# A four-layer kernel's Mamba scan stage: order of dt's projection, D times u and the decays of paired states

## What is computed

```python
u, z = split(xn @ in_w.T)                # 256 channels each
u    = silu(causal_conv4(u) + conv_b)
dbc  = u @ xproj_w.T                     # 64 columns for dt, 16 for B, 16 for C
dt   = softplus(dbc[..., :64] @ dt_w.T + dt_b)
dA   = exp(dt[..., None] * A)            # A: 256 x 16
dBu  = (dt * u)[..., None] * B[:, :, None, :]
h    = dA * h + dBu                      # over time, for each of 16 states
y    = sum_n(h * C) + u * D
out  = (y * silu(z)) @ out_w.T
```

## Time and profile before

| | us |
|---|---|
| median of the runs | 1367.63 |
| the profiled execution, span | 1397.4 |
| scan stage in it, first times_c to the last instruction of GpSimd's part | 44.4 to 808.0 |
| PE, DVE, ACT, POOL busy, whole span | 1272.1, 1097.7, 947.2, 1013.4 |
| one full unit of the scan stage, from GpSimd's times_c(11) to the next | about 47.6 |
| 40.00 to 810.00: PE, DVE, ACT, POOL busy | 728.79, 726.25, 668.12, 742.17 |

### The profile page before, as it was taken

One profiled execution on the slowest core, in us unless ns is written; L12 is line 12 of the kernel. 1 busy time (PEld: TensorE's weight loads), 2 busy tenths in 40 slices (PEclk: granted clock), 3 DMA queues, 4 the chain that ended last, 5 costly groups with the idle time before them and its releaser, 6 DMA issues.

```text
span 1397.4 us, 27753 instructions
## 1 busy us (share of the span) xinstructions
PE 1272.1 (91%) x9894; PEld 962.1 (69%) x9894; DVE 1097.7 (79%) x1829; ACT 947.2 (68%) x1630; POOL 1013.4 (73%) x620
## 2 busy tenths in 40 slices
PE   6799999999999999999998779999989999986695
PEld 2567767676777676766766646689966666656693
DVE  5799999999999999999999953333357888874475
ACT  5888988898889888988988842245545555532243
POOL 2789999999999999999999916223334665664442
PEclk9999999999999999999999999999999999998798
DMA  5545434543444454444444351312152000021223
GB/s 187 145 131 161 138 139 118 161 149 129 139 139 165 133 150 139 164 132 152 139 146 111 114 216 47 90 44 86 56 157 86 2 1 1 13 64 34 79 72 100
DMA packets 153014, 154.73 MB, mean 111 GB/s; under 512 B 96624, under 2 KB 121712, under 8 KB 143168
## 3 DMA queue, kind: packets, MB, share of 16 engines
q1 hardware_dynamic: 148112, 143.16, 32.8%
q0 software_dynamic: 4768, 9.81, 2.2%
HBM read 138.66 MB, written 20.20 MB: 114 GB/s over the span
## 4 chain that ended last, share of the span: by engine, by line
PE 49%; ACT 21%; DVE 16%; issue 8%; another core or an unknown queue 2%; DMA 2%; POOL 1%; SPq 1%; DVEq 1%; POOLq 0%; ACTq 0%
DVE hh L887 7%; PE pq L410 6%; ACT da L720 6%; PE pa L506 4%; PE py L525 3%; ACT pa L725 3%; PE bank L1562 3%; PE bank L1558 2%; PE pr L2016 2%; PE bank L1572 2%; PE pr L2219 2%; PE pr L2030 2%; PE bank L1478 2%; DVE hh L897 2%
## 5 line engine op out<-in xcount | busy, mean ns | idle before, releaser
L1042 POOL TENSOR_TENSOR hc<-hh,cs 128x1024 f32<-128x1024 f32 x256 | 596.9, 2369 | 24.6 <-DVE hh L887 21.7
L887 DVE TENSOR_TENSOR_SCAN hh<-da,st,pa 128x512 f32<-128x512 f32 x240 | 292.7, 1261 | 14.1 <-PE pa L506 12.6
L525 PE MATMUL py<-ident,hc 128*128 128x128 f32 x2048 | 268.4, 277 | 7.4 <-ACT yt L738 5.8
L525 PEld LDWEIGHTS py<-ident,hc 128*128 128x128 f32 x2048 | 229.1, 141 | 54.4 <-issue 29.1
L506 PEld LDWEIGHTS pa<-dg,dtut 64*128 64x128 f32 x2560 | 160.9, 189 | 107.0 <-issue 103.2
L506 PE MATMUL pa<-dg,dtut 64*128 64x128 f32 x2560 | 189.8, 285 | 29.6 <-DVE hh L887 20.6
L720 ACT ACTIVATE da<-dt,w 128x512 f32<-128x512 f32 x320 | 209.7, 711 | 0.2
L897 DVE TENSOR_TENSOR_SCAN hh<-pa,st,hh 128x512 f32<-128x512 f32 x144 | 175.2, 1265 | 6.1 <-POOL hh L1032 3.7
L725 ACT ACTIVATE pa<-dt,w 128x512 f32<-128x512 f32 x192 | 124.5, 680 | 35.2 <-DVE hh L887 20.8
L410 PE MATMUL pq<-xn,w 128*128 128x512 f32 x248 | 124.6, 627 | 3.6 <-ACT xn L755 3.6
L1032 POOL TENSOR_TENSOR hh<-dtu,bs 128x1024 f32<-128x1024 f32 x48 | 112.8, 2365 | 3.1 <-issue 1.9
(11 more groups left out here) (341 smaller groups left out, 2643.8 us busy)
## 6 DMA issues: line engine op xcount, KB each, us to landing
cs<-bcrows SPq DMA_DIRECT2D x64, 1024.0 KB, 4.9
dg<-blocks SPq DMA_DIRECT2D x80, 256.0 KB, 5.0
bs<-bcrows SPq DMA_DIRECT2D x48, 256.0 KB, 3.7
blocks<-bcrows SPq DMA_DIRECT2D x320, 1.0 KB, 3.2
xsorted<-in_pads SPq DMA_DIRECT2D x13, 387.0 KB, 5.7
rot<-in_rot SPq DMA_DIRECT2D x4, 1024.0 KB, 4.9
wx<-in_l_w SPq DMA_DIRECT2D x4, 1024.0 KB, 10.0
ysort<-ytoken SPq DMA_DIRECT2D x14, 256.0 KB
```

The costliest lines, as they stand in the source:

```text
L525: i = pe.matmul(py[:, h * CH + kt * P:h * CH + (kt + 1) * P], hc[s % HCS][:, h, t], ident[:, :], is_transpose=True, start=n == 0 and kt == ...
L887: v.tensor_tensor_scan(hh[(NS * m + nj) % HHS][:, h, :], da[q % DAS][:, :], inflows, 0.0 if first else st[:, m % 2, nj, h:h + 1], ALU.mult ...
L1042: g.tensor_tensor(hc[s % HCS][:, :, :], hh[s % HHS][:, :, :], cs[j % 2][:, s % CG, :].unsqueeze(1).broadcast_to([P, HF, CH]), ALU.mult).th ...
```

## The change

D*u goes from step 13 of TensorE to step 7, and from step 12 of ScalarE to step 5. `dt_project` and `relu_abs` come one step earlier each. The decays of pairs count on a semaphore of their own (`s_da`, which later serves `pad_zeroed` too, with its counts raised by `zero0`), have eight tiles instead of four, and are written at places given by two tables: DECAYS_FIRST before prep, DECAYS_LATE behind it. ScalarE's order from step 4 on becomes: keep_sum; keep_rows; decays 5, 6; relu_abs first half; u_times_d; decays 7; relu_abs second half; decays 8, 9; sigmoid; square 1; decays 11; square 2; decays 10, 12; square 3; decays 14; relu_again; keep_pre; decays 13, 15.

```diff
+DECAYS_FIRST = {0: (1,), 1: (2, 3), 3: (4,), 6: (7,), 8: (11,), 9: (10,), 10: (12,), 11: (14,), 12: (13, 15), 15: (16,)}
+DECAYS_LATE = {4: (5, 6), 6: (8, 9)}
...
-SLOTS, DAS, BG = 4, 4, 2
+SLOTS, DAS, BG = 4, 8, 2
...
+        s_zero, zero0 = sem("pair_decayed_then_pad_zeroed"), UNITS * 4 * len(PAIRS)
...
+            s_da = s_zero
...
-                by_tensor = [item[0] == "y" for item in handed_items]
+                elsewhere = [item[0] in ("y", "flow") for item in handed_items]
...
-                DD_AT = 9
+                DD_AT = 3
...
(TensorE's prep)
-                            if n in (5, 6):
-                                dt_project(m, n - 5)
+                            if n in (4, 5):
+                                dt_project(m, n - 4)
...
(ScalarE's prep)
-                            if n in (6, 7):
-                                relu_abs(m, n - 6)
-                            if n == 7:
-                                sigmoid(m)
+                            if n in (5, 6):
+                                relu_abs(m, n - 5)
...
-                        if n == 12:
+                        if n == 5:
                             u_times_d(m - 1)
                         if m < UNITS:
-                            if n in (8, 9, 10):
-                                square(m, n - 8)
+                            if n in (7, 8, 10):
+                                square(m, (7, 8, 10).index(n))
...
-                                act.activation(da[q % DAS][:, :], dt[m % 2][:, h, :], ACT.Exp, scale=wd[m % 2][:, a:a + 1]).then_inc(s_slot, 1)
+                                act.activation(da[q % DAS][:, :], dt[m % 2][:, h, :], ACT.Exp, scale=wd[m % 2][:, a:a + 1]).then_inc(s_da, 1)
...
(ScalarE's loop over the steps)
-                        ahead = s + 1 < STEPS and by_pe(s + 1) and BY_P.index((s + 1) % NS) % 2 and (s + 1) % NS < 10
-                        if s + 1 < STEPS and not ahead:
-                            decays(s + 1)
+                        for n in DECAYS_FIRST.get(s % NS, ()):
+                            if s // NS * NS + n < STEPS:
+                                decays(s // NS * NS + n)
...
-                        if s % NS == PAIRS[0][0] - 1:
-                            decays(s + 2)
...
                         prep(s // NS + 1, s % NS)
+                        for n in DECAYS_LATE.get(s % NS, ()):
+                            decays(s // NS * NS + n)
+                        if s % NS == 6 and s // NS + 1 < UNITS:
+                            sigmoid(s // NS + 1)
...
-                        if s % NS in [own[0] - 1 for own in PAIRS[1:] if own[1] < 10]:
-                            decays(s + 2)
...
(VectorE's scan)
-                                v.wait_ge(s_slot, slot_count(i))
+                                v.wait_ge(s_da, q + 1)
```

More of the change, by code:

```diff
@@ L301, in layer0_mamba @@
                 turn = {item: i for i, item in enumerate(handed_items)}
-                by_tensor = [item[0] == "y" for item in handed_items]
+                elsewhere = [item[0] in ("y", "flow") for item in handed_items]
                 def slot_count(i):
-                    return i + 1 - sum(by_tensor[:i + 1])
+                    return i + 1 - sum(elsewhere[:i + 1])
                 def dt_count(m):
@@ L1202, in build @@
         s_ht, s_yo, s_ys = sem("hidden_made"), sem("y_made"), sem("y_kept")
-        s_zero = sem("pad_zeroed")
         routed = {"route": 0}
@@ L1623, in tiles_scalar @@
                     act.wait_ge(s_re, 32)
-                    act.wait_ge(s_zero, 1)
+                    act.wait_ge(s_zero, zero0 + 1)
                     kept_up(0)
@@ L1668, in tiles_vector @@
                     v.wait_ge(s_re, 32)
-                    v.wait_ge(s_zero, 1)
+                    v.wait_ge(s_zero, zero0 + 1)
                     kept_gate(0)
```

## The result

The kernel after takes 1388.16 us (median of 4 runs, 1383.78 to 1393.36), the kernel before 1366.33 (4 runs, 1364.85 to 1369.02): a ratio of 1.0154, 95% interval 1.0125 to 1.0184, or 21.8 us (17 to 25) slower. The forecast was 1381 with a range to 1387; the sign, the ring and its parts were right, the sum was 7 us short. The four runs of before in this batch are on the low side: 61 further runs of it have a median of 1368.7, and against that after is 19.5 us slower. The profiled execution of after took 1390.27 us, with a span of 1388.1 and a granted clock of 0.982.

The account below looks back on a forecast made before the run. The prediction took a GpSimd and VectorE ring of 47.6 us a unit as the bound, replaced after the change by ScalarE's at 48.55; 14 times +0.95, 13.3 us, on 1367.6 gave 1381 us, range 1371 to 1387.

Parts of the forecast that it names:

- the ring: Scan stage, ScalarE's decays of 1 to 10, VectorE's steps 10 and 11, then back: 48.55 us a unit against 47.6.
- the sum: Whole stage: 14 rings at +0.95 us each, 13.3 us, put on the median 1367.6, giving 1381.
- Three small terms ... They cancel: Stage total: +0.35 in unit 0, up to -0.7 for faster scans, up to +0.5 where those don't count; net nothing.
- term for unit 0: Unit 0 of the scan stage: +0.35 us, because the decays of 10 come late there too.
- term for the units with faster scans: Units where a sequence begins and scans carry no initial state: up to -0.7 us off the loss.
- T: Time from ScalarE's decays of step 1 to the end of the first relu_abs's abs: 15.84 us.
- the waits named for the changed profile: Expected: VectorE before step 10 (0.5 to 0.8 us) and step 6 (1.5), TensorE before second dt_project (0.7 to 1.0), GpSimd 2.
- ScalarE's ring ... 45.8, 1.8 us under the present unit: Kernel before: ScalarE's loop through the decays of 10 takes 45.8 us, leaving 1.8 us of slack under 47.6.
- All that ScalarE costs VectorE in it is ... 0.17: GpSimd and VectorE's loop, kernel before: VectorE waits 0.17 us for the decays of 9; gain at most 2.4 us.
- Rival D: TensorE idles in each unit and drops to its lower clock: another 1 us a unit, +28 us, 1395; chance 0.03.
- A's two prices: Bounds of the main forecast (chance 0.74): costlier draining before loads +0.2 us a unit; D*u freeing 1.04, better overlaps -0.3.
- E's further stall: Rival: one more stall of 0.3 to 0.5 us a unit in TensorE's steps 8 to 10, 1386; chance 0.06.

Follow-up runs that it names:

- after again: The changed kernel, unchanged, run and profiled a second time; 1387.77 us, one run.
- before again: The kernel before, unchanged, run and profiled a second time; 1363.96 us, one run.
- dt back: The changed kernel with dt_project, relu_abs, sigmoid and squares at their old steps; 1370.93 us, 1.0014 against the kernel before.
- the decays alone: The kernel before with only the pairs' own semaphore, eight tiles and new tables of decay steps; 1383.19 us, 1.0098 against the kernel before.
- the run with the decays of 10 first: The changed kernel with the decays of 10 written ahead of those of 11; 1387.08 us, one run.
- dt alone: The kernel before with only dt_project and relu_abs one step earlier; 1409.77 us, 1.0282 against the kernel before.
- before a third time: The kernel before, unchanged, run and profiled a third time; 1373.11 us, one run.

## Why the prediction was right and where it was wrong

The step that failed is the sum over the stage, "Three small terms ... They cancel", and not the ring. Its term for unit 0 was +0.35 and measured 2.0; its term for the units with faster scans was up to -0.7 and came out at +0.8; and a time that goes with a lower granted clock was no term of it at all.

- **The ring was right, by its mechanism.** 48.55 forecast, 48.62 to 48.65 measured; T, the start of step 6 behind T, the decays of 10, steps 10 and 11 and the stretch behind them each within 0.1 us. Against 47.60 the 14 rings make 14.6 us in the first pair of profiles and 14.3 in the second (after again against before again), where 13.3 had been the sum. That the ring passes through step 10, and that dt and out_project make it longer, is shown by the runs that take parts of this away: 47.88 with D*u in step 6 and the decays of 10 first, 47.65 with dt back. Of the waits named for the changed profile, those before step 6, for the first relu_abs and of GpSimd came, and that for inflow 7 went. The one before step 10 came as add_out's wait for TensorE, in place of a wait for the decays: the prediction had both at about T + 14, and the decays lost by 0.1.
- **"ScalarE's ring ... 45.8, 1.8 us under the present unit"** failed. It summed ScalarE's instructions up to the decays of 10 and left out its wait for gate ahead of the decays of 7 (most of 1.1 us), and that VectorE, on its way from the decays of 9, comes to step 10 another 0.8 us later. The ring through the decays of 9 measured 47.57. For the whole change this did no harm, since relu_abs and u_times_d fill ScalarE's wait for gate there and the longer way to the decays of 10 decides. For the parts it was wrong: the decays alone cost 0.9 a unit and not 0.
- **"All that ScalarE costs VectorE in it is ... 0.17"** was right as a number and wrong as a reason. Taking it away wins 0.2 (47.41), and taking away GpSimd's inflow wins nothing (47.57): two rings ended together, which a small wait doesn't show.
- **"Three small terms ... They cancel"** failed. Unit 0 costs 2.0 us in the mean, not 0.35. The 0.35 counted the decays of 10; the wait seen in unit 0 of after again is 1.55 before the second dt_project. That this wait makes the 2.0 is argued and not shown: it is also 1.55 in the run with the decays of 10 first, but absent in after's first profile, where TensorE was late itself, and with unit 0's dt at its old step it is still 0.87. The faster scans were to take up to 0.7 off. In the two rings before and behind the row at 462.11 before goes down to 46.99 and 47.16, but after only to 48.34 and 48.49: these two lost 1.34 each and the others about 1.0, so the term has the other sign. The rings, faster scans included, and unit 0 make 14.6 + 2.0 = 16.6.
- **The rest goes with the clock**, a term that the sum hadn't at all. The time of before itself goes with the mean granted clock of the execution: of 61 runs beside the experiments the 12 with 0.979 to 0.982 have a mean of 1372.5 us, the 11 with 0.988 or 0.989 one of 1365.6. At 0.982 after has 1389.4 (four runs, 1386.1 to 1393.4) against 1372.9 (three), at 0.988 1383.78 (one) against 1366.5 (seven): 16.5 and 17.3, near the 16.6. But after is at 0.982 in four of five runs. Of all 17 runs whose dt in unit 0 is a step sooner 12 are at 0.982 or below, four of them dt alone with its many waits; of the 124 others, with the old step, 26. So the lower clock is more frequent with the early dt, and an estimate of what this adds at the median is up to 4 us (before's own: 1368.7 over all 61, 1372.5 at the low clock). It overlaps with the 2.0, since unit 0 is one of the places where the clock falls. Rival D had the clock in the middle units. In after's first profile it is 1.00 from 65 to 760; it falls in unit 0, at the end of unit 14 (0.50 in 765 to 770; before a third time has 0.50 in 750 to 755) and in the last unit. Dt alone, with its longer waits, does have it in the middle as well (0.80 in 615 to 620). Whether the lower clock makes these executions longer or both follow from waits elsewhere, and why the early dt should make it more frequent, by its idle 1.55 us in unit 0 or otherwise, wasn't tried and stays open.
- **The range** ended at 1387 because its bounds were those of the rings only (A's two prices and E's further stall). The 1388.16 is 1 us outside. 1367.6 with 16.6 and 4 is 1388, but that sum was made after the result and takes the clock at its upper figure.
- **Table loads.** In after the square that starts at 310.80 and lasts 1.15 is followed by the load at 311.97, 1.17 behind its start. The sum had 1.04 for the square, which is its length less the usual overlap, and 0.1 for draining: within 0.03 of it. The decays follow 0.01 behind the load. The drain of some 1380 ns for each switch, which the Trainium skill names (ScalarE: Activation LUTs, What ACT_TABLE_LOAD costs), does not show here either: by that page, an estimate, four of them would make the ring about 54 us.

## What to carry to other kernels

Where two engines seem to bound a loop, write out every ring that passes through each of them, with the waits for third engines inside it, and compare them at each place where two meet; a ring that is 0.1 us shorter is not slack. Moving work on an in-order engine is priced by what it then stands in front of: the three parts here, D*u, the decays and dt, cost -0.2, +0.9 and +2.8 us a unit alone and +1.0 together. And the first and the last pass of a loop want a sum of their own: here unit 0 took 2.0 us more where the prediction had 0.35.

## What the runs showed of the hardware

- The mean granted clock of a one-core kernel differs from execution to execution, from 0.979 to 0.989 over 61 runs of before, and 7 us of 1368 go with it.
- 8 transposing matmuls of add_up in unit 0 take 1.09 us at full clock in before run again and 1.97 in after's window of 0.50, as these rows of their TensorE timelines show, before again first:

```profile
52.11 1.09 PE L525 MATMUL py<-ident,hc 128*128 128x128 f32 x8 [0.62 <-ACT xn L755]
```

```profile
56.79 1.97 PE L529 MATMUL py<-ident,hc 128*128 128x128 f32 x8
```

- One profiled execution of before had 29.7 us of ScalarE's waits put down to "remote" that none of its repetitions had. A single profile's span is no base for a sum.
